# The gated recurrence input made by VectorE in one instruction, with the orders of four engines written anew

## What is computed

```python
r_t = jax.nn.sigmoid(x_conv @ W_r.T + b_r)
i_t = jax.nn.sigmoid(x_conv @ W_i.T + b_i)
a_t = a_base[None, None, :] ** (8.0 * r_t)
inp = i_t * x_conv
scale = jnp.sqrt(jnp.clip(1.0 - a_t * a_t, 0.0))
...
    h = a * h + b        # a = a_t, b = scale * inp
```

## Time and profile before

| | |
|---|---|
| median of 3 runs | 1268.12 us |
| the profiled execution | 1264.64 us |
| its span | 1262.7 us |
| mean granted clock of TensorE | 0.982 of full |
| TensorE busy | 1190.1 us, 94% |
| VectorE busy | 879.3 us, 70% |
| ScalarE busy | 718.8 us, 57% |
| GpSimd busy | 582.8 us, 46% |

### The profile page before, as it was taken

How to read it: one execution, slowest core, us unless ns; L and a number is a source line. 1 busy time by engine, 2 the same in 40 slices (tenths; PEclk the granted TensorE clock), 3 DMA queues, 4 the chain that set the end, 5 groups by cost and what they waited for, 6 DMA issues and landing times. The chain is left out here.

```text
span 1262.7 us, 17104 instructions
## 1 busy us (share of the span) xinstructions
PE 1190.1 (94%) x5812; PEld 930.9 (74%) x5812; DVE 879.3 (70%) x1494; ACT 718.8 (57%) x1116; POOL 582.8 (46%) x529
## 2 busy tenths in 40 slices
PE   5699999999999999999998989999999999999982
PEld 2487787886877868778776768778778688688871
DVE  7998976668466656775988987687666757555335
ACT  2455463563745646456566768667677474573633
POOL 4326653437144261255575728458463716224015
PEclk9799999999999999999998999999999999999996
DMA  7012154557466346666231115774645654736534
GB/s 209 17 35 50 18 176 120 164 143 210 156 189 179 106 126 184 195 179 179 68 84 17 34 27 171 194 192 126 175 131 157 197 162 136 220 104 202 153 91 134
DMA packets 113031, 170.79 MB, mean 135 GB/s; under 512 B 10025, under 2 KB 86577, under 8 KB 112945
## 3 DMA queue, kind: packets, MB, share of 16 engines
q1 hardware_dynamic: 94864, 124.59, 30.9%
q0 software_dynamic: 12320, 39.86, 15.8%
q10 hardware_dynamic: 5760, 5.25, 1.2%
HBM read 138.20 MB, written 16.27 MB: 122 GB/s over the span
## 5 line engine op out<-in xcount | busy, mean ns | idle before, releaser
L2272 PE MATMUL psum<-fwv,hid 128*128 128x256 f32 x1024 | 239.2, 380 | 2.0 <-ACT hid L1247 2.0
L2272 PEld LDWEIGHTS psum<-fwv,hid 128*128 128x128 f32 x1024 | 189.9, 190 | 31.9 <-ACT hid L1247 3.9
L788 POOL TENSOR_TENSOR rstd<-varis,half_neg 128x4 f32<-128x4 f32 x64 | 94.0, 1468 | 161.2 <-DVE varis L3193 109.4
L2313 PEld LDWEIGHTS psum<-xst,ew 128*128 128x128 f32 x1024 | 123.6, 192 | 8.0 <-issue 3.3
L2313 PE MATMUL psum<-xst,ew 128*128 128x128 f32 x1024 | 125.0, 275 | 0.8 <-ACT xst L1330 0.6
L905 POOL DMA_INDIRECT xs<-xf_rows,token_of_slot x40 | 52.6, 1316 | 142.6 <-PE psum L2301 122.1
L2321 PE MATMUL psum<-ew,hidt 128*128 128x256 f32 x512 | 115.9, 379 | 2.5 <-DMA ew<-in_w 1.8
L1243 ACT ACTIVATE hid<-psum 128x512 f32<-128x512 f32 x128 | 75.3, 595 | 63.4 <-PE psum L2193 43.2
L792 POOL TENSOR_SCALAR xhat<-rows_ring,negmean,rstd 128x256 f32<-128x256 f32 x108 | 103.6, 969 | 15.7 <-PE psum L2182 9.5
L2321 PEld LDWEIGHTS psum<-ew,hidt 128*128 128x128 f32 x512 | 96.8, 190 | 18.0 <-ACT hidt L1343 2.9
L1343 ACT ACTIVATE hidt<-psum 128x512 f32<-128x512 f32 x80 | 47.8, 598 | 93.4 <-PE psum L2313 79.8
(11 more groups left out here) (307 smaller groups left out, 2552.1 us busy)
## 6 DMA issues: line engine op xcount, KB each, us to landing
ew<-in_w SPq DMA_DIRECT2D x64, 1024.0 KB, 5.7
ew<-in_w SPq DMA_DIRECT2D x64, 512.0 KB, 4.7
rows_ring<-bias_rows POOLq DMA_DIRECT2D x28, 512.0 KB, 5.8
rows_ring<-in_x SPq DMA_DIRECT2D x14, 512.0 KB, 6.7
rows_ring<-y POOLq DMA_DIRECT2D x14, 512.0 KB, 5.2
out<-rows_ring SPq DMA_DIRECT2D x14, 512.0 KB, 6.4
rows_ring<-space POOLq DMA_DIRECT2D x12, 512.0 KB, 6.2
ys_rows<-ys ACTq DMA_DIRECT2D x40, 128.0 KB, 4.2
```

The source lines that it names most:

```text
L788: pool.tensor_tensor(dst, src, half_neg[:, 0:src.shape[1]], ALU.pow).then_inc(done, 1)
L2272: last = nc.tensor.matmul(rows4[:, k, :], hid[:, j % NHID, k * P:(k + 1) * P], fwv[:, j, :], start=j == 0 and k % 2 == 0, stop=j == FC - 1 ...
L2313: last = nc.tensor.matmul(bank_e[:, j * P:(j + 1) * P], ew1[:, c, at:at + P], xst[:, c, :], start=c == 0, stop=c == DC - 1)
```

## The change

ScalarE no longer makes 0.5 tanh + 0.5. VectorE takes the tanh and makes (tanh + 1) times the convolution's output in one scalar_tensor_tensor, for all 16 positions; this is twice the gated input. The logarithm of root_of takes a scale of -0.25 in place of -1, so that the root comes out half as large. GpSimd's gated_input is gone, and so are the constant half, its memset and the step "w".

Besides, the lists of GpSimd, ScalarE, TensorE and VectorE are written anew in nearly every turn; SyncE's stays as it is. Outside of gated_input no call is added or removed on any engine. Which position runs in which turn, and where tiles stand, is unchanged.

```diff
-        half = sb("half", [P, 1])
...
-        gates_out = steps("gates_out", numbered("r", DC) + numbered("i", DC) + ["w"], B)
+        gates_out = steps("gates_out", numbered("r", DC) + numbered("i", DC), B)
...
-            sp.wait_ge(consts_made, 5)
+            sp.wait_ge(consts_made, 4)
...
-            pool.memset(half[:], 0.5).then_inc(consts_made, 1)
...
-            def gated_input(p):
-                s = rec_sets[set_of(p)]
-                pool.wait_ge(gates_out.sem, gates_out.count(p, "w"))
-                pool.wait_ge(conv.sem, conv.count(p, "c01"))
-                pool.tensor_tensor(s.ig[:], s.ig[:], s.cv[:], ALU.mult).then_inc(gin.sem, 1)
...
-                act.wait_ge(gates_out.sem, gates_out.count(p, "i1"))
-                nc.scalar.activation(s.ig[:], s.ig[:], ACT.Identity, bias=half[:], scale=0.5).then_inc(gates_out.sem, 1)
...
-                nc.scalar.activation(s.om[:], s.om[:], ACT.Ln, scale=-1.0).then_inc(root.sem, 1)
+                nc.scalar.activation(s.om[:], s.om[:], ACT.Ln, scale=-0.25).then_inc(root.sem, 1)
...
             def gated_input(p):
                 s = rec_sets[set_of(p)]
-                dve.wait_ge(gates_out.sem, gates_out.count(p, "w"))
+                dve.wait_ge(gates_out.sem, gates_out.count(p, "i1"))
                 dve.wait_ge(conv.sem, conv.count(p, "c01"))
-                nc.vector.tensor_tensor(s.ig[:], s.ig[:], s.cv[:], ALU.mult).then_inc(gin.sem, 1)
+                nc.vector.scalar_tensor_tensor(s.ig[:], s.ig[:], 1.0, s.cv[:], ALU.add, ALU.mult).then_inc(gin.sem, 1)
```

VectorE's list in the middle (turn 9's end, turns 10 and 11):

```diff
                 residual_mid(9)
+                split_taps(5)
                 second_stats(9)
-                split_taps(5)
                 merge(0, 1)
                 mixed_key(10)
+                third_stats(6)
                 mixed_value(10)
                 mixed_receptance(10)
-                third_stats(6)
+                gated_input(5)
+                scales(5)
                 weights_ahead(10)
-                scales(5)
                 second_differences(9)
                 channel_mix_key(9)
                 channel_mix_receptance(9)
 
             def turn_10():
-                stats_in(11)
                 recur(5)
                 channel_mix_low(9)
+                weights_decayed(10)
+                stats_in(11)
+                mean_square(5)
                 weights_now(10)
-                weights_decayed(10)
-                mean_square(5)
-                gated_values(8)
-                combine(8)
                 finish(5)
                 beta_sums(10)
-                decayed_values(10)
+                gated_values(8)
                 denominators(10)
                 taps(6)
-                third_stats(7)
+                combine(8)
+                decayed_values(10)
                 split_taps(6)
                 weighted_values(10)
                 alpha_sums(10)
                 numerators(10)
                 gated(10)
                 first_differences(11)
+                third_stats(7)
                 mixed_key(11)
-                mixed_value(11)
                 residual_mid(10)
                 second_stats(10)
+                mixed_value(11)
                 scales(6)
+                gated_input(6)
+                experts_norm_first(1)
                 mixed_receptance(11)
-                experts_norm_first(1)
                 recur(6)
...
                 channel_mix_receptance(10)
                 weights_ahead(11)
                 experts_norm(1)
-                channel_mix_low(10)
 
             def turn_11():
                 gated_values(9)
+                gated_input(7)
                 experts_rows(1)
                 scales(7)
+                channel_mix_low(10)
+                combine(9)
                 weights_decayed(11)
```

GpSimd's list of turn 10, TensorE's around rec_products(5), ScalarE's and VectorE's in the tail, and VectorE's in the start:

```diff
             def turn_10():
-                gated_input(6)
-                keep2(10)
                 norm2(10)
                 scaled_input(6)
+                keep2(10)
                 mean_power(6)
                 residual(6)
 
             def turn_11():
...
             def turn_10():
                 value_columns(10)
                 recept_columns(10)
                 channel_value(8, 6)
-                channel_value(8, 7)
                 freed(ev2, 9, "e1")
                 rec_products(5)
                 channel_key(9, 0)
                 channel_key(9, 1)
+                channel_value(8, 7)
                 channel_key(9, 2)
-                channel_value(9, 0)
-                channel_key(9, 3)
                 freed(fin, 5, f"f{TC - 1}")
                 transposes_rec(6)
+                channel_key(9, 3)
+                channel_key(9, 4)
+                channel_value(9, 0)
                 channel_value(9, 1)
...
                 gelu_of(39, 1)
+                rows_back(39)
                 decay_gates_out(15)
-                rows_back(39)
                 input_gates_out(15)
                 nc.scalar.preload_act_table_set(LOG_EXP)
                 decays(15)
...
                 scales(15)
                 scaled_input(15)
                 recur(15)
+                merge_bias(1)
                 merge(1, 0)
                 residual(14)
...
-                decayed_values(0)
+                weighted_values(0)
                 alpha_sums(0)
-                weighted_values(0)
+                route_counts()
                 numerators(0)
                 gated(0)
                 first_differences(1)
...
                 split_weights(1, fwk[1], fwk_whole, fwk[0])
 
             def turn_1():
-                route_counts()
                 second_differences(0)
                 channel_mix_key(0)
```

More of the change, by code:

```diff
@@ L978, in turn_5, with turn_6 @@
                 next_gather(5, "a")
-                keep3(1)
                 norm1(6)
                 next_gather(4, "d")
+                keep2(5)
+                scaled_input(1)
+                norm2(5)
                 next_gather(5, "b")
[L983 to L986, removed]
                 keep1(6)
                 norm3(2)
+                next_gather(6, "a")
+                keep3(1)
                 mean_power(1)
+            def turn_6():
+                norm1(7)
+                residual(1)
                 next_gather(5, "c")
-            def turn_6():
-                keep3(2)
[L994 to L1003, removed]
+                norm2(6)
+                keep2(6)
+                scaled_input(2)
+                next_gather(6, "c")
+                next_gather(6, "b")
+                keep1(7)
+                keep3(2)
                 norm3(3)
@@ L1010, in turn_7 @@
                 residual(2)
-                gated_input(3)
-                keep3(3)
+                norm2(7)
+                scaled_input(3)
                 next_gather(7, "b")
@@ L1015, in turn_7, with turn_8 @@
                 keep2(7)
-                norm2(7)
-                scaled_input(3)
+                keep1(8)
+                norm3(4)
+                keep3(4)
                 mean_power(3)
+                residual(3)
+            def turn_8():
+                norm1(9)
+                next_gather(8, "b")
                 next_gather(8, "a")
[L1020 to L1028, removed]
+                scaled_input(4)
                 keep2(8)
                 norm2(8)
-                scaled_input(4)
                 keep1(9)
@@ L3067, in turn_15 @@
                 channel_key(14, 5, 13)
+                channel_value(14, 2)
                 tile_in(35)
@@ L3692, in turn_4, with turn_5 @@
                 mixed_key(5)
-                scales(0)
+                mixed_value(5)
                 residual_mid(4)
-                merge_bias(0)
-                mixed_value(5)
+                gated_input(0)
                 second_stats(4)
                 mixed_receptance(5)
-                gated_values(3)
                 recur(0)
-                combine(3)
-                third_stats(1)
                 second_differences(4)
                 channel_mix_key(4)
+            def turn_5():
+                channel_mix_receptance(4)
+                channel_mix_high(4)
+                weights_ahead(5)
+                gated_values(3)
+                combine(3)
@@ L3737, in turn_5, with turn_6 @@
-                recur(1)
-                third_stats(2)
-            def turn_6():
-                channel_mix_high(5)
-                weights_ahead(6)
-                channel_mix_low(5)
-                mean_square(1)
-                stats_in(7)
-                finish(1)
+            def turn_6():
+                stats_in(7)
+                channel_mix_high(5)
+                mean_square(1)
+                channel_mix_low(5)
+                finish(1)
+                channel_mix_receptance(5)
+                weights_now(6)
+                merge_bias(0)
@@ L3754, in turn_6 @@
                 weighted_values(6)
+                numerators(6)
+                gated_input(2)
                 denominators(6)
-                numerators(6)
```

1418 lines of the change are left out of this document (708 added, 710 removed).

## The result

The changed kernel took 1256.81 us (median of four runs, 1256.28 to 1258.64) beside 1268.09 for the kernel before, a ratio of 0.9925, 95% interval 0.9906 to 0.9944. Repeated later it was 1256.54 beside 1266.37, 0.9916 (0.9901 to 0.9932). The ratios put the gain at 9.5 and 10.6 us, the two pairs of medians at 11.3 and 9.8, where 5.1 had been forecast. Laid on the median of 1268.12, the ratio gives 1258.6, just inside it. The profiled execution took 1256.28 us, 8.4 less than the one before.

The account below looks back on a forecast made before the run. TensorE, busy 1190.1 of 1262.7 us, was taken as the bound, so only start, middle and tail could gain; -4.5 - 1.1 + 0 + 0.5 = -5.1 took the median from 1268.12 to 1263.0 us, range 1258 to 1270.5.

Parts of the forecast that it names:

- The middle: 640 to 760 us, where the expert tiles have run out: -4.5 us, bounds 0 and -5.9.
- Step 1: Middle, recur(5) ahead of stats_in(11): scans 3.7 us earlier, hole before rec_products(5) some 1.3, 3.0 more if the clock stays up.
- Step 2: Middle, recur(6): scales(6) 5.9 us earlier, but GpSimd's queue before scaled_input(6) may leave 3.3; 4.5 taken.
- The shift: ScalarE's instruction at 1232.48 us in position 15's chain: without it all that follows in the tail moves up 1.15 us.
- The tail: Position 15's chain: 1.15 us gained without the shift, merge_bias(1) 0.1 late; -1.1 us, bounds -1.3 and +0.5.
- The full stretches: Where TensorE is busy 80.00 of 80 us: a rewritten order can only open a hole; +0.5 us, bounds 0 and +2.
- sign of being wrong: TensorE's full stretches: the prediction is wrong if they show under 79.5 of 80 us.
- The start: route_counts moves ahead of numerators(0) on VectorE: 0 us, bounds -1 and +1.5.
- (2): GpSimd's norm3(7) and norm2(10) starve beside busier VectorE, scaled_input(6) no earlier, the middle gives nothing: 1267.5 us; 24%.
- (3): VectorE becomes the bound of the middle, three new instructions in series, +3.7 us there: slower, 1271.2 us; 16%.
- (4): Middle: three GpSimd products each held VectorE up for their whole 2.50 us; gain 6.7 there, 1260.8 us; 10%.

Follow-up runs that it names:

- scan5_behind_stats: The changed kernel with stats_in(11) ahead of recur(5) again on VectorE, nothing else; 1258.76 us, 0.9943 of the kernel before.
- middle_products: The kernel before with only the products of positions 5, 6 and 7 moved from GpSimd to VectorE, shift and orders kept; 1262.78 us, ratio 0.9973.
- shift_kept: The changed kernel with ScalarE's shift and the logarithm's old scale kept, VectorE making a plain product; 1262.29 us, 0.9961 of the kernel before.
- merge_bias_back: The changed kernel with merge_bias(1) back in turn 13 ahead of recur(11), out of the tail; 1256.51 us, 0.9927 of the kernel before.

## Why the prediction was right in sign and short in size

**The middle**, -4.5 with a bound of -5.9, measured -6.84. Step 1 held. The scans were to start 3.7 us earlier and did so by 3.9 (4.93 less the 1.01 of the start); the hole was to be 1.3 and was 0.73; the half clock went, 2.97 of the 3.0. Its reason was half wrong, and the 3.7 came out partly by luck: the slow mixes were to disappear and only moved, from 671.12 to 667.70. In their place VectorE lost less ahead of them: two waits for ScalarE, 1.61 us together before, are 0.28, and short rows of the norms take 0.9 us less. (Two slips of the working changed nothing: ScalarE loses 16 instructions, not 15, and half of 3.69 is 1.85, not 1.7.)

Step 2 is what failed, "the lead there may be only 3.3. Between 3.3 and 5.9 I take 4.5". It was too small at both ends. scales(6) was to come at most 5.9 us earlier and came 7.6 earlier (722.32 to 713.72, less the 1.01 of the start). The bound passed on VectorE's lead of 3.7 alone. But VectorE also waits for the squares of position 5, 3.09 us at 688.61, and these follow rec_products(5), which ended 6.9 us earlier, net of the start and with the 3.0 of half clock in it; so TensorE's gain reached VectorE too, and that wait is gone. This is read from the traces; scan5_behind_stats fits it, where hole, half clock and a wait of 3.76 us for the squares come back together. GpSimd's queue, in turn, was less of a brake than I took it for: the scalings of norm3(7) ran in 2.16 instead of 8.00 us, the statistics that norm2(10) waits for were there at 712.49 (722.41 before), and scaled_input(6) came 6.9 earlier, net of the start. middle_products puts the relief of the products by itself at 1.3 to 2.6 us, without any lead to pass on. How much of the 6.84 hangs on the 6.66 us of the one trace before isn't known: behind a hole of the same length middle_products took 5.34.

**The shift** was counted once, 1.15 in the tail. That is right there: rec_products(15) begins 8.97 us earlier and rec_products(14) 7.66, so 1.3, and 1.2 from shift_kept to the changed kernel. But it was given nothing elsewhere, and it has a price in the middle, 1.02 in the changed order; over the whole, shift_kept prices it at some 5 us, of which some 3 have no place yet.

**The tail**, -1.1, measured -0.94 in the last stretch and +0.08 in the repeat; what varies lies behind rec_products(15). merge_bias(1) fills a wait, shown by merge_bias_back. **The full stretches**, +0.5, measured +0.19 and in the repeat +1.68, with one wait of 2.21 us for weights at 1011 us. The prediction's own sign of being wrong, a full window under 79.5 of 80, is there twice, 79.01 and 77.79; but the kernel before has two such windows too, 79.37 from 160 to 240 us and 78.53 from 400 to 480, so the sign was badly set. **The start**, 0, measured -1.0 and in the repeat +0.4, which is no more than chance.

**The rivals.** (2), GpSimd starving, fell as a forecast: of the two steps that it named norm3(7) ran freely and norm2(10) took 3.86 us, which cost 1.6 of its lead of 9.45. Its mechanism is there all the same, in other scalings of the middle, at 658.88, 672.41 and 688.04 us, which took 7.71, 7.13 and 9.34 us; TensorE's transposes named none of them as what they waited for. (3), VectorE as the bound, is refuted by middle_products. (4), every product holding VectorE up for its whole length, asked for 6.7 us in the middle and 6.84 came, by another sum: stats_in(11) and the half clock are 3.59 of it, and the three products alone gave 2.60 at most where its terms ask for 3.8 (7.5 less 3.7). The Trainium skill (SBUF — State Buffer, "two separate sides") has whichever of the two engines starts first keep the other out for the whole instruction. The pair of rows above agrees as far as it goes: 2.12 us lost by the mixes in one run, 0.4 by GpSimd in the other. Not every neighbour pays: statistics of 1.40 us ran beside a product unslowed.

What no part of the prediction had is that the edit in the old order can be slower than before. "GpSimd issues the same DMAs, some in another place" passed over the queue: a product that waits 26 us also holds a transfer back for 26 us. The changed order avoids the collision at 483 us, worth 3.4 to 5.7; in the middle it adds 0.4 us to what the edit gives.

## What to carry to other kernels

When an instruction that waits long is taken out of a queue, list what stands behind it: each DMA there now starts earlier, and one that meets the loads TensorE needs next cost 3.4 to 5.7 us here. (It need not cost that much: at 1011 us the later transfer shortened the wait by some 2 us, and no gain in the whole could be shown.) When it is put into another queue, put it behind whatever doesn't need its input. Two calls set right did as much as four rewritten lists, within what the runs can tell, so look for the first new wait before writing an order anew.

## What was not expected of the hardware

A quarter of a microsecond decided over 2.1: the product started 0.64 us after the pair of mixes in one run and 0.88 in the other, and they took 3.53 and 1.41 us. The other traces agree. Where scaled_input(5) began 0.30 to 0.64 us after a pair (the kernel before, the changed one and its repeats, shift_kept, middle_products) the pair took 3.51 to 3.53; where it began 0.87 to 0.88 after (the three runs of the edit in the old order) the pair took 1.41 and the product 0.4 more than its 2.35. Two mixes take 1.41 us, so the early product falls into the first, and the second mix waits it out: each slowed pair ends 0.5 to 0.6 us behind the product's end. The late one falls into the second and waits for that itself, and the statistics behind the pair aren't slowed.

TensorE's sixteen matmuls took 6.66, 5.34 and 5.12 us behind holes of 3.28, 3.27 and 3.08 us, with a granted clock of 0.50 and of 0.59 from 676 to 680 us in scan5_behind_stats; behind holes of 0.57 to 1.23 they took 3.69, at 1.00. So a hole of 3 us costs 4.5 to 6.3 in all. Why the same hole of 3.3 us cost 3.0 more once and 1.7 the other time isn't shown.
